# Value rows repeated by DMA instead of spread by TensorE, and scans in four of every five slots

## The reference

```
x = x + 0.5 * ffn(layernorm(x))
x = x + attention(layernorm(x))
x = x + 0.5 * ffn(layernorm(x))

ffn:  probs = softmax(x @ router_w.T); the two largest of 8, normalised, are the gates
      h = relu(x @ w1[e].T + b1[e]);  y = h @ w2[e].T + b2[e];  out = sum of gate[e] * y
attention, per batch row, with 4 heads, 16 keys and 32 values a head:
      r, k, v, w, g from mixes of x with the token before it
      S_t = exp(-exp(w_t))[k] * S_(t-1) + k_t[k] * v_t[v]         (a state of 16 x 32 a head)
      o_t[v] = sum over k of q_t[k] * (S_(t-1) + u[k] * k_t[k] * v_t[v])
      o is normalised within its head, scaled, multiplied by silu(g), and goes through W_o
```

## Time and profile before

| what | before |
|---|---|
| three runs, median | 531.13 us (530.73 to 532.26) |
| the profiled execution | 532.41 us, span 530.6 us, mean granted TensorE clock 0.995 |
| TensorE products busy | 512.0 us, 96% |
| TensorE weight loads busy | 320.0 us, 60% |
| VectorE busy | 388.5 us, 73% |
| ScalarE busy | 304.5 us, 57% |
| GpSimd busy | 201.3 us, 38% |
| DMA | 25.70 MB, mean 48 GB/s |

### The profile page before, as it was taken

One profiled execution on the slowest core, in us unless ns is written; L12 is line 12 of the kernel. 1 busy time (PEld: TensorE's weight loads), 2 busy tenths in 40 slices (PEclk: granted clock), 3 DMA queues, 4 the chain that ended last, 5 costly groups with the idle time before them and its releaser, 6 DMA issues.

```text
span 530.6 us, 6194 instructions
## 1 busy us (share of the span) xinstructions
PE 512.0 (96%) x1946; PEld 320.0 (60%) x1946; DVE 388.5 (73%) x745; ACT 304.5 (57%) x481; POOL 201.3 (38%) x228
## 2 busy tenths in 40 slices
PE   7999999999999999999989999999999999999996
PEld 3566575565557545555745555566655557777774
DVE  3555388688849698886998899679789968784443
ACT  2766587642367654335775633288552338787773
POOL 0025421657611253763105276501527741112212
PEclk9999999999999899999999999999999999999999
DMA  6184111011101002010003011001101111003200
GB/s 227 52 296 183 40 41 40 3 40 41 40 0 41 1 1 80 40 41 1 2 1 119 2 41 40 17 25 41 60 2 40 40 41 55 6 1 119 61 0 20
DMA packets 10352, 25.70 MB, mean 48 GB/s; under 512 B 2640, under 2 KB 2768, under 8 KB 10192
## 3 DMA queue, kind: packets, MB, share of 16 engines
q1 hardware_dynamic: 10320, 25.32, 14.2%
HBM read 24.13 MB, written 1.18 MB: 48 GB/s over the span
## 4 chain that ended last, share of the span: by engine, by line
PE 48%; issue 21%; POOL 13%; DVE 12%; ACT 3%; DMA 1%; POOLq 0%; SPq 0%; DVEq 0%; ACTq 0%
PE Y L282 11%; PE U L261 7%; POOL qs L805 6%; PE U L263 6%; PE U L262 6%; POOL xT L789 4%; PE Y L277 3%; PE Y L278 3%; PE Y L279 3%; DVE hid_lo L655 3%; DVE pool_a L708 2%; DVE gy L664 1%; DVE xnt L590 1%; DVE aw L736 1%; POOL pool_a L811 1%
## 5 line engine op out<-in xcount | busy, mean ns | idle before, releaser
L484 ACT ACTIVATE hid<-U,small 128x512 f32<-128x512 f32 x152 | 104.4, 687 | 140.7 <-PE U L263 140.1
L789 POOL TENSOR_TENSOR xT<-xT,gy 128x512 f32<-128x512 f32 x64 | 83.7, 1308 | 228.3 <-DVE gy L664 228.1
L282 PE MATMUL Y<-hid,w 128*128 128x512 f32 x304 | 155.0, 591 | 0.0
L261 PE MATMUL U<-xhi,w1lo 128*128 128x512 f32 x256 | 140.6, 549 | 2.5 <-ACT hid L484 1.5
L655 DVE TENSOR_TENSOR hid_lo<-hid,hid_hi 128x512 fp32r<-128x512 f32 x104 | 77.4, 752 | 33.5 <-ACT hid_hi L482 32.9
L263 PE MATMUL U<-xhi,w1hi 128*128 128x512 f32 x256 | 101.0, 394 | 0.0
L262 PE MATMUL U<-xlo,w1hi 128*128 128x512 f32 x256 | 100.9, 394 | 0.0
L481 ACT ACTIVATE hid<-U,small 128x512 f32<-128x512 f32 x104 | 71.4, 687 | 42.0 <-PE U L263 37.7
L805 POOL TENSOR_TENSOR qs<-q,pool_a 128x512 f32<-128x512 f32 x64 | 75.9, 1187 | 27.4 <-DVE pool_a L691 27.4
L261 PEld LDWEIGHTS U<-xhi,w1lo 128*128 128x128 f32 x256 | 48.3, 189 | 55.0 <-issue 38.5
L482 ACT ACTIVATE hid_hi<-U,small 128x512 fp32r<-128x512 f32 x104 | 71.0, 682 | 0.0
(11 more groups left out here) (127 smaller groups left out, 554.6 us busy)
## 6 DMA issues: line engine op xcount, KB each, us to landing
G<-gate_dram SPq DMA_DIRECT2D x32, 512.0 KB, 3.8
pool_a<-wexp_dram SPq DMA_DIRECT2D x8, 256.0 KB, 5.4
w<-wexp_dram SPq DMA_DIRECT2D x8, 256.0 KB, 5.5
xT<-xT_dram SPq DMA_DIRECT2D x4, 256.0 KB, 6.2
qs<-const_dram SPq DMA_DIRECT2D x1, 1024.0 KB, 10.3
out_dram<-xT SPq DMA_DIRECT2D x4, 256.0 KB, 4.3
small<-small_dram SPq DMA_DIRECT2D x1, 656.0 KB, 8.3
gate_dram<-gate_T SPq DMA_DIRECT2D x32, 4.0 KB, 1.4
```

What stands on the lines that cost most here:

```text
L261: mm(dst, w1lo[:, e, f, :], xhi[:, k % NB, :], start=True, stop=False)
L282: mm(dst, w2[:, g % E, f, :], hid[:, n % HS, :], start=first, stop=final).then_inc(down, 1)
L484: act.activation(hid[:, n % HS, :], U[n % 2][:, :], ACT.Relu, bias=bias).then_inc(h_f, 1)
L789: pool.tensor_tensor(xT[:, h, b, :], xT[:, h, b, :], gy[:, g % 2, :], ALU.add).then_inc(acc, 1)
```

## The change

- **Values by DMA.** ScalarE copies v out of its bank as plain fp32 into `v`, in place of the high part `vhi`; the low part and VectorE's subtraction are gone. SyncE writes `v` (256 KB) twice to DRAM, so that each row lies there two times (`VD` = 2), waits for the landing, and fetches the first five tiles. A tile is 16 rows of 2 KB, each repeated 8 times, 256 KB in SBUF; `vb` holds five (`VS`). ScalarE issues the other eleven fetches of a unit, one after each of its copies 1 to 11 (`fetch`).
- **ScalarE in TensorE's place.** `show` copies tile m from `vb` to the bank of scan m, one slot ahead of the scan. It waits for the fetch, and for scan m - 3 as the spread did. `v_spread`, the matrix `sel` and its 1 MB load and conversion are gone. VectorE multiplies in the same bank as before, and waits for the copy.
- **Four scans in five slots.** `scan_at(t)` gives scans to four slots and leaves the fifth free: 20 slots from `T_SC` = 18. The reduces are at t = 24, 29, 34 and 39, three slots behind their last scan instead of two. `T_PO` goes from 34 to 40 and `T_OUT` from 44 to 48, and since `UNIT` keeps its distance of 42 slots the tail of a unit lies over the first slots of the next.
- **Fewer slots in parts.** `in_parts` now leaves out every slot from three before the scans to `T_OUT`, not `T_PO`: 68 slots are in parts in place of 104, and the other 36 take the plain fp32 product.
- **Preparations later.** `PREP` of blocks 4 to 7 is 119, 129, 170 and 212, before 114, 125, 167 and 208.
- **SyncE's list by slots.** The gate loads are single items placed by `gates_slot`, merged with `values` (slot `UNIT[i]` + 13) and the outputs.

```diff
--- before.py
+++ after.py
@@ -21,26 +21,27 @@
 EPS = 1e-5
-PREP = [None, 6, 34, 80, 114, 125, 167, 208]
+PREP = [None, 6, 34, 80, 119, 129, 170, 212]
 UNIT = [37, 79, 121, 163]
 LAG = 3
 EQ = 2
 NQ = E // EQ
 HS, QS, SS = 5, 8, 4
-FP, PS, GS = 3, 3, 6
+FP, PS, GS, VS = 3, 3, 6, 5
+VD = 2
 T_DEV, T_NRM, T_CHN, T_LO = 1, 2, 4, 5
 T_LG, T_EXP, T_RT = 6, 7, 8
-T_XM, T_Z, T_MUS, T_PR, T_SC = 5, 7, 9, 12, 16
-T_PO = T_SC + VG + 2
-T_VAR, T_NORM, T_OUT = T_PO + 2, T_PO + 3, T_PO + 10
+T_XM, T_Z, T_MUS, T_PR, T_SC = 5, 7, 9, 12, 18
+SC = 20
+T_PO = T_SC + SC + 2
+T_VAR, T_NORM, T_OUT = T_PO + 2, T_PO + 3, T_PO + 8
 MIX = (1, 0, 2, 3, 4)
-MUS_BANK, SPREAD_BANK = (0, 1, 2, 0, 1), (1, 2, 0)
+MUS_BANK, STATE_BANK = (0, 1, 2, 0, 1), (1, 2, 0)
 C_ID, C_RED, C_CEN, C_AVG, C_BET, C_TIE = 0, 128, 256, 384, 512, 640
-C_SEL = C_TIE + 64
-C_ALL = C_SEL + VG * P
+C_ALL = C_TIE + 64
@@ -51,6 +52,19 @@
+def gates_slot(k, c):
+
+    if k == 0 and c < GS // EQ:
+        return -1
+    return max(4 * (k * E + (c + 1) * EQ - GS) + 4, PREP[k] + T_RT + 5 if k else 0)
+
+
+def scan_at(t):
+
+    j = t - T_SC
+    return 4 * (j // 5) + j % 5 if 0 <= j < SC and j % 5 < 4 else None
+
+
 def layernorms():
@@ -76,7 +90,7 @@
-    scans = any(start + T_SC - 3 <= n < start + T_PO for start in UNIT)
+    scans = any(start + T_SC - 3 <= n < start + T_OUT for start in UNIT)
     return n >= SLOTS and n % FC < FP and not scans
...
@@ -135,8 +148,8 @@
         dec = sb("dec", [P, NT])
-        vhi = sb("vhi", [P, NT], F32R)
-        vlo = sb("vlo", [P, NT], F32R)
+        v = sb("v", [P, NT])
+        vb = sb("vb", [P, VS, NT])
         sg = sb("sg", [P, NT])
...
@@ -202,14 +215,26 @@
                                  gate_T[q4 * 32:q4 * 32 + 32, b, :]).then_inc(g_out[k], 16)
+
+            def gates_in(k, c):
+                at = (k * E + c * EQ) % GS
                 sp.wait_ge(g_out[k], 64)
+                if k * E + (c + 1) * EQ > GS:
+                    sp.wait_ge(comb, k * E + (c + 1) * EQ - GS)
                 rows = gate_dram[k // NB].rearrange("(b k e t) p -> b k (e t p)", b=NB, k=NQ, e=EQ)
-                for k4 in range(NQ):
-                    at = (k * E + k4 * EQ) % GS
-                    if k * E + (k4 + 1) * EQ > GS:
-                        sp.wait_ge(comb, k * E + (k4 + 1) * EQ - GS)
-                    sp.dma_start(G[:, at:at + EQ, :].rearrange("p e n -> p (e n)"),
-                                 rows[b, k4].partition_broadcast(P)).then_inc(g_in[at // EQ], 16)
+                sp.dma_start(G[:, at:at + EQ, :].rearrange("p e n -> p (e n)"),
+                             rows[k % NB, c].partition_broadcast(P)).then_inc(g_in[at // EQ], 16)
+
+            def values(i):
+                sp.wait_ge(v_r, i + 1)
+                for d in range(VD):
+                    sp.dma_start(v_dram[i].rearrange("(r d) n -> r d n", d=VD)[:, d, :], v[:, :]).then_inc(v_out[i], 16)
+                sp.wait_ge(v_out[i], 16 * VD)
+                for m in range(VS):
+                    n = i * VG + m
+                    if n >= VS:
+                        sp.wait_ge(vp, n - VS + 1)
+                    sp.dma_start(vb[:, n % VS, :], value_rows(v_dram[i], m)).then_inc(v_in[n % VS], 16)
@@ -221,23 +246,32 @@
             weights(1)
-            sp.dma_start(const[:, C_ID + P:C_SEL], const_in[:, C_ID + P:C_SEL]).then_inc(const_l, 16)
+            sp.dma_start(const[:, C_ID + P:C_ALL], const_in[:, C_ID + P:C_ALL]).then_inc(const_l, 16)
             rows_in(1)
             for e in range(2, 4):
                 weights(e)
             gates_to_rows(0)
+            for c in range(GS // EQ):
+                gates_in(0, c)
             for e in range(4, E):
                 weights(e)
             rows_in(2)
             sp.dma_start(w(0, W_RT), small_in[:, 0:W_RT]).then_inc(small_l, 16)
-            sp.dma_start(sel_raw, const_in[:, C_SEL:C_ALL]).then_inc(sel_l, 16)
             rows_in(3)
-            gates_to_rows(1)
-            for k in range(2, 6):
-                gates_to_rows(k)
-            for k in (6, 7):
-                rows_out(k - 2)
-                gates_to_rows(k)
+            for n in range(ALL):
+                for k in range(1, BLOCKS):
+                    if n == PREP[k] + T_RT + 5:
+                        gates_to_rows(k)
+                for k in range(BLOCKS):
+                    for c in range(NQ):
+                        if n == gates_slot(k, c):
+                            gates_in(k, c)
+                for i in range(UNITS):
+                    if n == UNIT[i] + T_PR + 1:
+                        values(i)
+                for k in (4, 5):
+                    if n == (k + 1) * SLOTS + 8:
+                        rows_out(k)
             for k in (6, 7):
@@ -341,21 +375,6 @@
                 mm(A[bank][:, :], w(at, P), u[:, c, :], start=True, stop=True).then_inc(pr, 1)
-
-            def v_spread(i, m):
-                if m >= 3:
-                    pe.wait_ge(st_r, i * VG + m - 2)
-                elif m == 0:
-                    pe.wait_ge(sel_r, 1)
-                    pe.wait_ge(vlo_r, i + 1)
-                    pe.wait_ge(bet_c, i + 1)
-                elif m == 1:
-                    pe.wait_ge(bv_r, i + 1)
-                else:
-                    pe.wait_ge(sg_r, i + 1)
-                dst, j = A[SPREAD_BANK[m % 3]][:, :], order(m)
-                mm(dst, sel[:, j, :], vlo[:, :], start=True, stop=False)
-                mm(dst, sel[:, j, :], vhi[:, :], start=False, stop=True).then_inc(vb, 1)
@@ -410,10 +429,8 @@
                     proj(i, 0, W_G, 4)
-                if T_SC <= t < T_SC + VG:
-                    v_spread(i, t - T_SC)
-                if T_SC + 5 <= t < T_SC + 5 + VG and (t - T_SC - 5) % 4 == 0:
-                    reduce(i, (t - T_SC - 5) // 4)
+                if T_SC + 6 <= t <= T_SC + SC + 1 and (t - T_SC) % 5 == 1:
+                    reduce(i, (t - T_SC) // 5 - 1)
                 if t == T_PO:
@@ -496,10 +513,33 @@
+            def fetch(i, m):
+                n = i * VG + m
+                act.wait_ge(vp, n - VS + 1)
+                act.dma_start(vb[:, n % VS, :], value_rows(v_dram[i], m)).then_inc(v_in[n % VS], 16)
+
+            def show(i, m):
+                n = i * VG + m
+                if m == 0:
+                    act.wait_ge(bet_c, i + 1)
+                if m == 1:
+                    act.wait_ge(bv_r, i + 1)
+                if m == 2:
+                    act.wait_ge(sg_r, i + 1)
+                if m >= 3:
+                    act.wait_ge(st_r, n - 2)
+                act.wait_ge(v_in[n % VS], 16 * (n // VS + 1))
+                act.activation(A[STATE_BANK[m % 3]][:, :], vb[:, n % VS, :], ACT.Copy).then_inc(vp, 1)
+
             def attend(i, t):
                 h, b = home(i)
                 if t == T_DEV:
                     deviation(LN_ATT[i])
+                m = scan_at(t + 1)
+                if m is not None:
+                    show(i, m)
+                    if m >= 1 and m + VS - 1 < VG:
+                        fetch(i, m + VS - 1)
                 if t == T_CHN:
@@ -522,7 +562,7 @@
                     act.wait_ge(pr, 5 * i + 4)
-                    act.activation(vhi[:, :], A[2][:, :], ACT.Copy).then_inc(vhi_r, 1)
+                    act.activation(v[:, :], A[2][:, :], ACT.Copy).then_inc(v_r, 1)
                 if t == T_PR + 2:
@@ -678,8 +718,8 @@
                 n, (h, b) = i * VG + m, home(i)
-                bank = A[SPREAD_BANK[m % 3]][:, :]
-                dve.wait_ge(vb, n + 1)
+                bank = A[STATE_BANK[m % 3]][:, :]
+                dve.wait_ge(vp, n + 1)
                 dve.tensor_tensor(bank, bank, kk[:, :], ALU.mult).then_inc(kv_r, 1)
@@ -712,17 +752,15 @@
                                              op0=ALU.mult, op1=ALU.mult).then_inc(quk_r, 1)
-                if t == T_PR + 1:
-                    dve.wait_ge(vhi_r, i + 1)
-                    dve.tensor_tensor(vlo[:, :], A[2][:, :], vhi[:, :], ALU.subtract).then_inc(vlo_r, 1)
                 if t == T_PR + 2:
+                    dve.wait_ge(v_r, i + 1)
                     dve.wait_ge(bet_c, i + 1)
                     dve.tensor_tensor(o[:, :], A[2][:, :], quk[:, :], ALU.mult).then_inc(bv_r, 1)
                     dve.wait_ge(sg_t, i + 1)
                     dve.scalar_tensor_tensor(out=sg[:, :], in0=sg[:, :], scalar=1.0, in1=A[0][:, :],
                                              op0=ALU.add, op1=ALU.mult).then_inc(sg_r, 1)
-                if T_SC <= t < T_SC + VG:
-                    scan(i, t - T_SC)
+                if scan_at(t) is not None:
+                    scan(i, scan_at(t))
                 if t == T_PO - 1:
...
@@ -827,8 +862,8 @@
                             seed_state(i, m)
-                if T_SC <= t < T_SC + VG:
-                    m = t - T_SC
+                m = scan_at(t)
+                if m is not None:
                     read_state(i, m)
@@ -850,6 +885,12 @@
     return 4 * c + n
+
+
+def value_rows(v_dram, m):
+
```

(27 more changed lines are left out.)

## The result

The changed kernel takes 518.92 us (median of four, 517.76 to 519.54), the kernel before on the same chips 531.09: a ratio of 0.9765, 95% interval 0.9740 to 0.9789. The profiled execution took 519.4 us with a span of 517.6 and a mean granted clock of 0.982, where before had 0.995. The forecast was 512.7 with a range of 504 to 525. Against the forecast's sum with nothing late, 506.2 for a profiled execution, 13.2 us came back, where I had forecast 7.8; one term alone, VectorE's backlog, came to 15.0, and others came out lower.

A forecast was written before the change was run, and what follows sets the result against it. TensorE's issue was taken as the bound: 532.4 us less 30.1 (spread) plus 5.8 (parts) less 1.9 (last reduces) gave 506.2; late terms of 3.4, 2.4, 1.0 and 1.0 gave 514.0, median 512.7, range 504 to 525.

The forecast's parts named there:

- nothing late: Whole kernel: 506.2 us profiled if no engine or load comes late; as a rival 504.9 us, chance 0.20.
- VectorE's backlog: First scans of units 2 and 3: block 5's and 6's routing overloads VectorE; +3.4 us, bounds 0 and 5.5.
- TensorE's issue is the bound: Scan stage: TensorE never idle; removing the spread takes scan slots from 2.02 to 1.55 us, -30.1 us.
- the clock: TensorE's granted clock falling after idle waits: -1.7 to +3.4 us, taken as 0.
- First value tile: Start of each unit's scans: tile 0 lands 1.7 us late after v's writes; 0.6 per unit, +2.4 us.
- Preludes: A unit's tail moves into the next unit's prelude, where VectorE was already late: +1.0 us, bounds -1 and +3.
- Gates: Gates of blocks 4 and 7 leave later; block 7's some 2 us late for its combine: +1.0 us (0 to 3).
- No gain: VectorE or something else sets the pace behind TensorE's full row: 531 to 533 us, chance 0.05.
- The value tile is late: v's write takes both turns, each unit loses 3.5 us instead of 0.6: 524 us, chance 0.12.
- The slower rival: Tile supply limits scans to one every L / 4; slower from L = 10 us, 564 us at 12; chance 0.06.

The follow-up runs named there:

- Experiment 3: Changed kernel's slots, preparations, parts and SyncE list, but v spread by TensorE as before, without value tiles or copies: 537.62 us, ratio 1.0107.
- Experiment 2: Changed kernel with 18 extra TensorE products into a free bank ahead of the first reduce in units 2 and 3: 513.26 us, ratio 0.9651.
- experiment 7: Changed kernel with units 2 and 3 three slots later (124, 166) and blocks 6 and 7 with them (173, 215): 511.90 us, ratio 0.9608.
- experiment 8: As experiment 7, but with unit 3 at 168 and block 7 at 217: 509.49 us, ratio 0.9567.
- experiment 1: Changed kernel with routing steps 3 to 5 of blocks 5 and 6 moved to slots without a scan: 514.34 us, ratio 0.9666.
- experiment 4: Kernel before's slots, preparations and parts (16 scans in 16 slots), with value tiles by DMA as in the changed kernel: 523.33 us, ratio 0.9831.

## Why the prediction was right or wrong

**TensorE's issue is the bound: right.** Slots with a scan went from 2.02 to 1.54 us, and in unit 0 the 22 slots from the first scan to the last reduce, with four reduces, take 39.3 us (109.5 to 148.8), where this pace gives 22 x 1.55 + 4 x 1.19 = 38.9. Experiment 3 puts the spread back and is 18.7 us slower, 30.1 less the waits and the low clock that it covers.

**The step that failed is VectorE's backlog in units 2 and 3**, +3.4 with bounds 0 and 5.5. The place was right, TensorE waiting at the first reduces of these units; the size was not. It was 15.0: 9.0 of waiting and about 6 of low clock. Three things in it were wrong. First, I summed VectorE's load over the whole stage, 35.3 + 3.7 against 35.8, where the wait is decided at the first reduce. From the combine at 290.04 VectorE had four scans, 5.5 us of routing and a combine to do, 14.1 us, and GpSimd's product behind them; the reduce was due at 300.76. But for the second point the load per unit was right; the window was wrong. Second, the three groups of block 5's routing took 5.5 us, not 3.7: in each, one small operation ran 0.90 to 1.30 us long (291.14, 294.70, 298.88), 3.3 us of the 5.5, and the row that I had taken for the last step held one such operation and those for the other two none; see below. Third, the clock was put at 0 with the reason that such waits "may go or come", beside a forecast that brought two of them. The row of before had the price, and it should have been charged to each new wait of some us. Experiment 2 shows this part, 5.7 us; experiments 7 and 8 show the backlog, as the waits fall to 1.4 us when the routing ends before the scans.

**First value tile: +2.4 forecast, 0 measured.** The two writes landed in 2.3 us each, not 4.3, which was the row of a write of the same size at another time. The Trainium skill, "DMA: Bandwidth & Descriptors", section "Anatomy of one DMA", has a fit for DMAs issued by GpSimd; an estimate from it is 2.6 us for 256 KB. The 2.3 us measured here, on SyncE's queue, lie near it. In unit 0 the first fetch was issued at 105.37 and the tile was copied at 109.21, so it landed in 3.8 us or less. That saved 2.4 us of the forecast, while the backlog's term lost 11.6.

**Preludes: +1.0 forecast.** Unit 1's got better (5.9 to 4.7) and unit 2's worse (3.3 to 7.1), +2.6 together. **Gates: +1.0 forecast, 0 here**: VectorE went into the combine of slot 135 at 281.22 without a wait. The mechanism was sound: experiment 8, with block 7 five slots later, paid 4.9 us for it in slots 235 and 236, which took 8.05 us against 3.17 in the changed kernel (I had put it at 5.3).

**The sum.** With these terms as measured, 506.2 + 15.0 + 0 + 2.6 + 0 = 523.8, and the execution took 519.4. The other 4.4 us had no term: some 2 are at block 4's preparation, 0.6 lie before the first slot (its up product starts at 10.85 instead of 11.49), and the rest I cannot place. So the mechanism was forecast and its size missed by a factor of over four; that the time lies within 504 to 525 owes something to luck, since 7.8 us that came out lower than forecast (first tile 2.4, gates 1.0, no term 4.4) stood against it.

**The rivals.** "No gain" and the rule of the weight-load share in the Trainium skill, "Perfetto Trace Analysis", section "Identifying the Most-Contended Engine", would have had the time stand still; weight loads went from 60 to 56% of the span while the time fell by 2.3%, and neither share tells that TensorE's issue ran without a gap in two stages of four. "The value tile is late" is out by ScalarE's group. The slower rival did not show with five tiles, and decides with two.

## What to carry to other kernels

When the bounding engine is relieved, sum the next engine's load up to each point where the first one waits for it, not over the stage; a load that is fine on the average can be 5 us over at the first of such points. Price a new idle of TensorE with the lower clock that may follow: each wait of 2.99 us and more in these runs was followed by it, and so were some of the shorter ones. And an offload and the order that goes with it are two terms: here the offload alone gave 1.7%, the new order on top of it 0.7, and moving the units clear of the routing 2.0 more (2.5 with block 7's routing and the last tail), while the new order alone was a loss of 1.1.

## What the runs showed of the hardware that I had not expected

**Small VectorE operations stretched beside GpSimd.** A comparison of 128x32 elements takes VectorE 0.19 us at most places and 1.30 at 294.70; GpSimd's product of the same kernel after ran from 294.68 for 1.28.

```profile
294.68 1.28 POOL L840 TENSOR_TENSOR qs<-q,pool_a 128x512 f32<-128x512 f32 x1 [2.28 <-DVE pool_a L731]
```

The same is to be seen with other small operations at 382.07 (1.30, GpSimd from 382.02 for 1.31) and 388.07 (1.08, GpSimd from 387.85 for 1.27): the small operation ends with GpSimd's, to 0.05 us. The kernel before has it at 394.51 (1.07, GpSimd from 394.27 for 1.28), so that the 1.93 us of a last routing step in the earlier trace rows held 0.9 of such waiting. I did not test it; that the two wait for one another is read from these coincidences alone.

**The clock.** The two waits of 4.85 and 4.19 us were each followed by some 6.8 us at the lower level (at half speed, the 0.42 missing from 8 us in experiment 2's first window is 6.7 us of it). Some 3.4 us of it followed waits of 2.13 and 2.20 (experiment 1), 2.19 (unit 2's prelude after), 2.10 and 2.99 (experiment 4), 3.08 (experiment 8), also the 3.95 of unit 3 in experiment 7, and the 1.26 of the kernel before. None followed those of 2.65 and 2.35 in experiment 4, of 2.22 in unit 2's prelude in experiment 1, and of 2.02, 1.41 and 1.40 in experiments 3 and 7. The length of the wait alone does not decide; what else does stays open.

**Landing times.** A 256 KB tile of repeated rows took 3.7 us in the median but up to 9.4; four in flight hid even that.
